# Two attentions and two expert layers on one core: new places for the last batches, the logits, and the third shared result

## The reference

```python
x = x + tanh(g_xattn[0]) * L0_xattn(layernorm(x), ctx)   # 16 heads, projections Wq, Wk, Wv, Wo with biases
x = x + tanh(g_ffn[0])   * L0_ffn(layernorm(x))          # 32 experts, 4 per row, at most 128 rows each, + shared
x = x + tanh(g_xattn[1]) * L1_xattn(layernorm(x), ctx, ctx)   # 8 heads, no projections
x = x + tanh(g_ffn[1])   * L1_ffn(layernorm(x))          # 8 experts, 2 per row, + a shared network
```

## Time and profile before

| | before |
|---|---|
| median of 3 runs | 773.63 us (771.66 to 774.16) |
| the profiled execution | 771.27 us, of which the span is 769.5 us |
| mean granted TensorE clock | 0.959 of 2.4 GHz |
| busy: PE, DVE, ACT, POOL | 668.0, 523.1, 368.9, 343.6 us |
| chain that ended last | PE 54%, DVE 17%, issue 9%, POOL 6%, DMA 5% |

### The profile page before, as it was taken

One profiled execution on the slowest core, in us unless ns is written; L12 is line 12 of the kernel. 1 busy time (PEld: TensorE's weight loads), 2 busy tenths in 40 slices (PEclk: granted clock), 3 DMA queues, 4 the chain that ended last, 5 costly groups with the idle time before them and its releaser, 6 DMA issues.

```text
span 769.5 us, 13735 instructions
## 1 busy us (share of the span) xinstructions
PE 668.0 (87%) x4737; PEld 347.7 (45%) x4738; DVE 523.1 (68%) x1248; ACT 368.9 (48%) x612; POOL 343.6 (45%) x401
## 2 busy tenths in 40 slices
PE   3889999999999999778845699999887999897996
PEld 1233333333333356667512344445332566565763
DVE  3788888898887599435267799998636832332336
ACT  2057777877778354234413566666402213333420
POOL 3836465564412100655367887520100067666530
PEclk9999999999999999979966999999969999999999
DMA  6945454565522660245644778877511022222137
GB/s 157 196 114 138 129 141 131 158 179 151 156 65 67 200 179 14 67 122 149 209 128 127 206 217 236 221 197 194 161 46 29 0 68 81 73 67 74 49 94 265
DMA packets 111708, 101.12 MB, mean 131 GB/s; under 512 B 26517, under 2 KB 95802, under 8 KB 111512
## 3 DMA queue, kind: packets, MB, share of 16 engines
q1 hardware_dynamic: 99872, 76.19, 35.4%
q0 software_dynamic: 8352, 18.74, 8.6%
q10 hardware_dynamic: 3416, 5.31, 2.8%
HBM read 58.49 MB, written 24.40 MB: 108 GB/s over the span
## 4 chain that ended last, share of the span: by engine, by line
PE 54%; DVE 17%; issue 9%; POOL 6%; DMA 5%; SPq 4%; another core or an unknown queue 2%; ACT 2%; ACTq 0%; POOLq 0%; DVEq 0%
PE S L425 9%; PE O L470 9%; PE ST L1537 5%; DVE mx L589 5%; POOL spare L297 3%; PE ST L433 3%; PE ST L1463 2%; PE M L1554 2%; PE S L1554 2%; PE M L519 2%; PE ST L957 2%; PE M L512 2%; SPq L174 2%; DMA QS<-mxT 1%
## 5 line engine op out<-in xcount | busy, mean ns | idle before, releaser
L589 DVE TENSOR_REDUCE mx<-S 128x2 f32<-128x512 f32 x384 | 250.9, 684 | 34.8 <-PE S L425 33.1
L345 ACT ACTIVATE PX<-ST 128x1024 f32<-128x1024 f32 x192 | 196.2, 1024 | 92.0 <-PE ST L433 84.6
L425 PE MATMUL S<-QS 62*128 62x256 bf16 (+1 forms) x768 | 150.7, 292 | 39.5 <-DVE mx L589 26.0
L433 PE MATMUL ST<-QS 64*128 64x256 bf16 (+1 forms) x768 | 140.0, 276 | 1.4 <-DMA QS<-mxT 1.1
L470 PE MATMUL O<-PX,VA 128*32 128x256 f32 x1536 | 122.3, 391 | 0.3 <-DMA VA<-in_val 0.2
L425 PEld LDWEIGHTS S<-QS 62*128 62x128 bf16 (+1 forms) x768 | 47.7, 97 | 157.4 <-DVE mx L589 95.3
L297 POOL DMA_INDIRECT spare<-ye,GI x64 | 67.7, 1058 | 29.1 <-DMA ye<-QKc 14.8
L1648 POOL DMA_INDIRECT PX<-xn,TI x39 | 39.9, 1022 | 63.6 <-DVE K1n L1837 39.7
L800 POOL DMA_INDIRECT PX<-xn,TI x32 | 34.5, 1077 | 58.7 <-DVE spare L1186 44.1
L433 PEld LDWEIGHTS ST<-QS 64*128 64x128 bf16 (+1 forms) x768 | 53.3, 96 | 16.1 <-issue 9.0
L1537 PE MATMUL ST<-EGU,Cb 128*128 x156 | 54.7, 474 | 4.7 <-issue 2.9
(11 more groups left out here) (302 smaller groups left out, 1127.3 us busy)
## 6 DMA issues: line engine op xcount, KB each, us to landing
QS<-QKs SPq DMA_DIRECT2D x93, 128.0 KB
QS<-keys SPq DMA_DIRECT2D x16, 512.0 KB
keys<-spare SPq DMA_DIRECT2D x96, 64.0 KB
QS<-QKs SPq DMA_DIRECT2D x93, 64.0 KB
EGU<-in_ew SPq DMA_DIRECT2D x16, 256.0 KB, 2.7
xn<-spare SPq DMA_DIRECT2D x8, 512.0 KB, 5.7
ye<-QKc SPq DMA_DIRECT2D x32, 128.0 KB
VA<-in_val SPq DMA_DIRECT2D x16, 256.0 KB
```

The lines of the kernel that those rows point to most:

```text
L345: e.activation(M["PX"][pair % 4][:, :], M["ST"][pair % 2][:, :], ACT.Exp, scale=A.scale).then_inc(A.exp, 1)
L425: got = e.matmul(M["S"][n % 2][:, 256 * a:256 * a + 256], QS[:, 0, 128 * a:128 * a + 128], QS[:, 1, :], start=True, stop=True)
L433: got = e.matmul(M["ST"][(NP * t + k // 2) % 2][:, 512 * u + 256 * a:512 * u + 256 * a + 256], QS[:, 1, 128 * a:128 * a + 128], QS[:, 0, : ...
L589: e.tensor_reduce(M["mx"][b % 2][:, :, A.row_of_max(head)], M["S"][n % 2][:, :].rearrange("p (a s) -> p a s", a=2), AX.X, ALU.max, negate= ...
```

## The change

`LAST` gives the batches 13, 14 and 15 of the second attention positions of their own, counted as 8 `t` + `k`: for `reciprocals`, `denominators`, `normalized`, `output` and `added`. `NORMS` splits the last group of norms, batches 12 to 15, into 12, 13 and 14, 15. In both ends the transposes, logits and, in part, the first hidden chunks get earlier places between the chains of the last batches; in the second, ACT copies them and not DVE. In the first, some steps of `marks` come sooner. `down(2)` moves from before the routed experts to behind them, between `hidden` 13 and 14. The keys' loads for the stacks 2 and 3 (and the transfers `holes`) move from SP's end of the expert stage to behind batch 1's spreads.

```diff
+        self.holes = 0 if self.first else 32
...
+    LAST = {13: (120, 127, 127, 129, 130), 14: (128, 132, 133, 134, 135), 15: (136, 138, 139, 140, 141)}
     def late(self, b):
-        return not self.first and b < NB - 2
+        return not self.first and b not in self.LAST
+    def last(self, what, t, k):
+        return [b for b in self.LAST if self.LAST[b][what] == self.H * t + k]
...
-            if b1 == 0 and behind_first:
+            if b1 == (0 if A.first else 1) and behind_first:
...
-        w.wait_ge(A.ldc[b % U], 16 * ((A.n0 + b) // U + 1))
+        w.wait_ge(A.ldc[b % U], 16 * ((A.n0 + b) // U + 1) + A.holes)
...
-                if k == 1 and within(b6) and not A.late(b6):
-                    output(b6)
+                for b in A.last(3, t, k):
+                    output(b)
...
-                if k == 7 and within(b5) and not A.late(b5):
-                    denominators(b5)
+                for b in A.last(1, t, k):
+                    denominators(b)
...
+def stack_ready(e, w, B, M, d, b):
+    for k in range(2):
+        w.wait_ge(B.kept[k], 96 * NB // 2)
+    w.wait_ge(B.kept[2], 32)
+    keys_loaded(e, B, M, b)
+    for got in holes(e, M, d, B.stack(b), second=True):
+        got.then_inc(B.ldc[b % U], 16)
...
-    w.wait_ge(G.up, 4 * NGRP)
-    for b in (2, 3):
-        stack_ready(b)
...
+        if t == NB + 1:
+            roots(3)
         if t == NB + 2:
-            roots(3)
+            roots(4)
...
-        if g == 3:
+        if g % 2:
             w.wait_ge(A.exp, A.NP * NB)
         for a in range(2):
-            got = e.matmul(BK[5 if g == 3 else 1][0:E0, :], M["GW"][:, a, :], XT[:, a, 512 * g:512 * g + 512],
+            got = e.matmul(BK[5 if g % 2 else 1][0:E0, :], M["GW"][:, a, :], XT[:, a, 512 * g:512 * g + 512],
                            start=(a == 0), stop=(a == 1))
         got.then_inc(G.lr, 1)
@@ -845,22 +856,28 @@
     def at(t, k):
         if t == NB - 1 and k in (2, 5, 9, 13):
             transposed((2, 5, 9, 13).index(k))
         if t == NB:
...
+            if k == 3:
+                logit_rows(0)
             if k == 12:
-                logit_rows(0)
+                logit_rows(1)
             if k == 15:
-                logit_rows(1)
                 logits(0)
+                logits(1)
                 transposed(4)
         if t == NB + 1:
             if k == 1:
-                logits(1)
                 transposed(5)
+            if k == 3:
+                logit_rows(2)
+            if k == 13:
+                hidden(e, w, G, M, 0)
             if k == 15:
-                logit_rows(2)
-                hidden(e, w, G, M, 0, 1)
+                transposed(6)
+                hidden(e, w, G, M, 1)
         if t == NB + 2 and k == 15:
-            transposed(6, 7)
+            transposed(7)
...
 def ffn0_pe_later(e, w, G, M):
     w.wait_ge(G.er, E0)
-    hidden(e, w, G, M, 12, 13, 14, 15)
+    hidden(e, w, G, M, 12, 13)
     w.wait_ge(G.ey, E0)
+    down(e, w, G, M, 2)
+    hidden(e, w, G, M, 14, 15)
     down(e, w, G, M, 3)
     w.wait_ge(G.xs, NB)
-    w.wait_ge(G.late, 16 * (PLACES - EARLY + 2 * U))
...
-    down(e, w, G, M, 2)
...
         if t == NB + 1 and m == 0:
             sigmoids(0, 2)
-        if t == NB + 2 and m == 7:
+        if t == NB + 1 and m == 7:
             logit_rows(2)
             relu_squared(e, w, G, M, 0)
-            columns(6, 7)
+        if t == NB + 2 and m == 7:
+            columns(6)
             relu_squared(e, w, G, M, 1)
+            columns(7)
...
 def ffn0_act_later(e, w, G, M):
-    relu_squared(e, w, G, M, 12, 13, 14, 15)
+    relu_squared(e, w, G, M, 12, 13)
+    copied_out(e, w, G, M, 8, 12)
+    relu_squared(e, w, G, M, 14, 15)
...
-    copied_out(e, w, G, M, 8, 12)
...
-        if t == NB and k == 14:
-            logit_rows(0)
+        if t == NB:
+            if k == 12:
+                logit_rows(0)
+            if k == 14:
+                logit_rows(1)
         if t == NB + 1:
-            if k == 0:
-                logit_rows(1)
+            if k == 1:
                 columns(4, 5)
+            if k == 2:
+                marks(4)
+            if k == 14:
+                statistics(3, rows(12, 14))
+                marks(1)
             if k == 15:
-                rows(12, 15)
+                rows(14, 15)
                 marks(1)
         if t == NB + 2 and k == 15:
-            statistics(3, rows(15, 16))
-            marks(1)
             normed_rows(3)
+            statistics(4, rows(15, 16))
+            marks(2)
+            normed_rows(4)
...
+        if t == -1 and k == 3:
+            shared_added(e, w, G, M, 2)
...
-        if x == E0 // 2:
-            shared_added(e, w, G, M, 2)
...
+NORMS = ((0, 4), (4, 8), (8, 12), (12, 14), (14, 16))
...
         if t == NB:
             if k == 3:
                 logit_rows(0)
+                transposed(4)
+            if k == 4:
+                logits(0)
+                logit_rows(1)
+            if k == 5:
+                transposed(5)
+            if k == 6:
+                logits(1)
+                logit_rows(2)
+        if t == NB + 1:
+            if k == 0:
+                w.wait_ge(M["w_f1"], M["n_f1"])
+                shared_hidden(e, w, G, M, 0)
+            if k == 2:
+                logits(2)
+            if k == 3:
+                transposed(6)
+            if k == 4:
+                shared_hidden(e, w, G, M, 1)
             if k == 7:
-                logit_rows(1)
-                logits(0)
-                transposed(4)
-        if t == NB + 1:
-            if k == 1:
-                logits(1)
-                transposed(5)
-            if k == 7:
-                logit_rows(2)
-        if t == NB + 2 and k == 1:
-            w.wait_ge(M["w_f1"], M["n_f1"])
-            shared_hidden(e, w, G, M, 0)
-            transposed(6, 7)
-            logits(2)
-            logit_rows(3)
-            logits(3)
+                transposed(7)
+                logit_rows(3)
+                logits(3)
...
-    shared_hidden(e, w, G, M, 1, 2)
+    shared_hidden(e, w, G, M, 2)
...
-        if t == NB + 2 and m == 1:
+        if t == NB and m == 1:
+            logit_rows(0)
+            columns(4)
+            logit_rows(1)
+            columns(5)
             logit_rows(2)
+        if t == NB + 1 and m == 1:
             columns(6, 7)
             logit_rows(3)
...
-        if t == NB + 2:
+        if t == NB:
             roots(3)
+        if t == NB + 1:
+            roots(4)
...
-            if k == 7:
+        if t == NB:
+            if k == 1:
                 columns(3)
-        if t == NB and k == 7:
-            logit_rows(0)
+            if k == 3:
+                statistics(3, rows(12, 14))
         if t == NB + 1:
-            if k == 2:
-                logit_rows(1)
-                columns(4, 5)
-            if k == 7:
-                rows(12, 15)
-        if t == NB + 2 and k == 7:
-            statistics(3, rows(15, 16))
-            normed_rows(3)
+            if k == 1:
+                normed_rows(3)
+                rows(14, 15)
+            if k == 5:
+                statistics(4, rows(15, 16))
+            if k == 6:
+                normed_rows(4)
...
+            def columns_left():
+                w.wait_ge(X.up, 4 * NGRP)
+                for b in (2, 3):
+                    stack_ready(e, w, L1, M, d, b)
+            attention_sp(e, w, L1, M, lambda e, w, n: rows(n), columns_left)
```

More of the change, by code:

```diff
@@ L668, in attention_dve @@
                     statistics(bn)
-                if k == (4 if A.late(b5) else 0) and within(b5):
+                if k == 4 and within(b5) and A.late(b5):
                     reciprocals(b5)
+                for b in A.last(0, t, k):
+                    reciprocals(b)
                 if k == 2 and within(t - 4) and A.late(t - 4):
                     added(t - 4)
-                if k == 2 and within(b6) and not A.late(b6):
-                    added(b6)
+                for b in A.last(4, t, k):
+                    added(b)
                 if k == {-2: 7, -1: 3}.get(t, 2) and within(b0):
@@ L690, in attention_dve @@
                     normalized(b6)
-                if k == 7 and within(b5) and not A.late(b5):
-                    normalized(b5)
+                for b in A.last(2, t, k):
+                    normalized(b)
             meanwhile(t, k)
@@ L746, in ffn0_sp @@
     e.dma_start(rows[:, :, T:ROW0], M["wd"]).then_inc(G.wrow, 16)
-    def stack_ready(b):
-        for k in range(2):
-            w.wait_ge(B.kept[k], 96 * NB // 2)
-        w.wait_ge(B.kept[2], 32)
-        keys_loaded(e, B, M, b)
-        for got in holes(e, M, d, B.stack(b), second=True):
-            got.then_inc(G.late, 16)
     for x in range(E0):
@@ L1198, in rows, with statistics, normed_rows @@
         return got
-    def statistics(g, last):
+    def statistics(n, last):
+        lo, hi = NORMS[n]
         last.then_inc(G.bn, 1)
-        w.wait_ge(G.bn, 3 * g + 1)
```

(20 more changed lines are left out.)

27 lines of the change are left out of this document (12 added, 15 removed).

## The result

| | before | changed |
|---|---|---|
| median of 11 runs | 771.66 us (762.34 to 774.16) | 777.53 us (774.46 to 780.86) |
| ratio, with its 95% interval | | 1.0114 (1.0087 to 1.0141) |
| span of the profiled execution | 769.5 us | 775.5 us |
| mean granted clock | 0.959 | 0.953 |

The kernel is slower by 6 to 11 us. The ratio is taken over the fast runs alone; the quotient of the two medians is 1.0076.

A forecast was written before the change was run, and what follows sets the result against it. VectorE and TensorE, nearly always busy in the second attention, leave late batches no room; TensorE fills both ends at low clock. 2.0 − 0.3 + 4.9 + 0 + 0.7 = +7.3 us on the 773.63 median: 780.9 us, range 775.0 to 786.0.

The forecast's parts named there:

- the late denominators: Sign in the first attention's end: denominators(15) start 3 us later, with logit rows just ahead of them.
- the parts behind the copies: Sign at the second attention's start: ScalarE's parts and spreads of the first batch stand behind the copies of down(3).
- TensorE idle ahead of the chunk: Sign in the last end: TensorE idles before the first shared chunk until the last weights load; 4 us idle forecast.
- First attention's end: Reordered work at the first attention's end starts the experts' gathers later: +2.0 us (0.8 to 2.7).
- Routed experts: Expert stage without down(2) ahead: TensorE starts sooner but then waits for gathers, −0.3 us (−1.7 to 0).
- Rival (4): Routed experts: 11.7 us of unnamed waits go when TensorE starts with the gathers; 769.5 us, chance 0.09.
- Second attention's start: Behind the experts, down(2) delays ScalarE's first-batch parts and spreads, so scores(0) start +4.9 us later (3.0 to 5.5).
- Rival (2): Second attention's start: ScalarE's order doesn't matter, something else holds the first batch; 4.9 us less, 776.0 us, chance 0.10.
- Keys' loads: Two loads moved to run beside the second attention's gathers cost 0 us (0 to 1.8).
- Second attention's end: Earlier logits gain, but the first shared chunk waits for the last expert's weights: routing +0.7 us (−2.3 to +2.5).
- it ends at 554.2, 2.1 later: Second attention's end: the last product, with output(13) and two more groups ahead of it, ends 2.1 us later.
- Rival (3): Second attention's end: the last weights aren't late, the end gains its full −4.6 us; 775.6 us, chance 0.08.

The follow-up runs named there:

- e5: The changed kernel itself, run again on the second chip against the kernel before: 754.56 us, ratio 1.0143.
- e9: The kernel before, run against itself on the third chip for a trace: 744.38 us, ratio 1.0018.
- e2: The changed kernel with down(2), its copies and its sum back ahead of the routed experts: 746.64 us, ratio 1.0029 to the kernel before.
- e6: The changed kernel with the second attention's first-batch parts and spreads ahead of down(3)'s copies on ScalarE: 753.64 us, ratio 1.0139 to the kernel before.
- e3: The changed kernel with the keys' loads of stacks 2 and 3 ahead of the second attention again: 752.29 us, ratio 1.0101 to the kernel before.
- e1: The changed kernel with the last expert's two weight loads ahead of ScalarE's five copies again: 745.82 us, ratio 1.0037 to the kernel before.
- e11: The kernel before with only the change's second attention's end, last expert's loads behind the copies: 747.25 us, ratio 1.0039.
- e8: The kernel before with only the change's second attention's end, last expert's loads ahead of the copies: 738.76 us, ratio 0.9931.

## Why the prediction was right

The forecast was +7.3 us, slower; measured were +5.9 us between the medians on the first chip (+8.8 by the ratio) and +10.7 in e5. The signs that the prediction named for itself are in the traces: the late denominators, the gathers at 313.76 (forecast 313.4), the parts behind the copies, TensorE idle ahead of the chunk. The closeness of the sum is in part luck. Put alone on the kernel before, the parts cost 1.3 to 2.1 us (first end), 7.7 (down(2)) and 2.9 (last end), 12 to 13 together, where the terms are 2.0, 4.9 − 0.3 and 0.7; the whole change costs less than they add to, and why that is was not tried. By its steps:

- **First attention's end, +2.0 (0.8 to 2.7).** Measured 2.4 in the first pair of traces, 1.5 in the means of all traces, 1.3 to 3.8 by the times. The clock was low during the third logit rows (3.37 us for four matmuls), as the upper bound had it. Right.
- **Routed experts, −0.3.** The stage took 60.7 us against 60.8, and no gain rises above the spread of 50 to 55 us of the others. The size is right, the reason only in part: in the changed kernel TensorE waits for the first gather already, where I had it catch up after six, and the prediction did not count the clock of 0.50 behind those waits, to which the rest of the 7 us may have gone. Rival (4) fell, that the unnamed waits of 11.7 us come from TensorE's late start and that the time goes down with them. Their share in the changed kernel's chain on the first chip is 9.1% of 59 us, 5.4 us, so 6.3 us less, but the stage is no shorter; and e9, the kernel before, has none in its chain.
- **Second attention's start, +4.9.** At scores(0) it was 4.4 on the first chip. Measured alone in the changed kernel (e2) it is 5.6 at scores(0), 4.4 to 7.4 at the last product and some 8 at the end. The place and the size at scores(0) are right, the size at the end was too small; the cause was told too narrowly. ScalarE's order holds the first batch, as I said, but e6 shows that with it mended TensorE's 7 us bound the same place 2.4 us earlier, and nothing of these 2.4 us shows at the end. Rival (2) fell.
- **Keys' loads, 0 (0 to 1.8).** Beside the gathers they cost 2.4 us or more on one chip (157.7 us in e3, 160.1 in e1), which is above the bound of 1.8, and little or nothing by traces of other chips; and they win 2.2 at scores(0), because the barrier no longer waits for them, which the prediction left out. The two errors cancel, so that 0 stands by luck. By the Trainium skill, "DMA: Bandwidth & Descriptors", section "Issuing engines are not separate DMA queues", transfers started by ScalarE, SyncE and GpSimd run on the same DMA engines and interleave; the faster stage of e3 (157.7 us) agrees; what I would have added by it, 0.7, is within what the traces leave open.
- **Second attention's end, +0.7 (−2.3 to 2.5).** The step itself, the chunk's wait for the last expert's weights, was 4.74 us where I had 4, with the low clock behind it. As a sum it was too small by the middle value: e11 measures +2.9 us (0.5 to 5.3), and its trace has 3.8 in B and 0.3 in C. The term that was mis-sized is the start, "it ends at 554.2, 2.1 later": the last product came 3.8 us later (B, e11 against e9, on one chip). The forecast of the sum stopped at the routing and left out the 1.1 us won behind it. Rival (3), that the end gains in full, fell, but e8 shows that it is to be had.

Open are the size of the first end (1 to 4 us), the cause of 1.1 to 2.4 us of the last end's B, and whether the keys' loads cost anything beside the gathers.
